# Tiles of the second layer by turns wide and narrow, a gather ring of 63 rows, and graph 2 ranked too, in a two-layer graph network kernel

## The reference

```python
# layer 0
scores = jnp.where(adj != 0, -jnp.arange(N), -jnp.inf)      # the first 25 neighbours
vals, idx = jax.lax.top_k(scores, 25)
agg = jnp.where(valid, x[idx], -inf).max(axis=2)            # elementwise maximum of their rows
agg = jnp.where(degree <= 25, jnp.maximum(agg, 0), agg)     # degree = sum of the adjacency row
x1 = layernorm(x + relu(concat([x, agg]) @ W0 + b0))
# layer 1, 8 heads of 32
Wh = x1 @ W
e = leaky_relu(s1[i] + s2[j] + edge_emb[1], 0.2)            # only where adj[i, j] is 1
alpha = softmax(e over the neighbours)
h = sum_j alpha[i, j] * Wh[j]
out = layernorm(x1 + elu(layernorm(h) * gamma + beta))
```

## Time and profile before

| what | us |
|---|---|
| median of 3 runs (lowest, highest) | 3435.09 (3434.90, 3439.38) |
| the profiled execution, its own time | 3435.9 |
| its span | 3434.2 |
| POOL busy | 2484.3 (72%) |
| DVE busy | 2417.8 (70%) |
| PE busy | 1578.9 (46%) |
| ACT busy | 1114.7 (32%) |
| POOL idle before its ring gathers, put down to "issue" | 705.0, in 2217 pieces |

### The profile page before, as it was taken

The page is one execution under the profiler, slowest core; times in us unless marked ns, Lnnn a source line. Parts: engine busy times, 40 slices in busy tenths (PEclk is TensorE's granted clock), DMA queues, the critical chain, the costliest instruction groups (busy, mean ns, idle before and its releaser), DMA issues. The chain is left out here.

```text
span 3434.2 us, 25542 instructions
## 1 busy us (share of the span) xinstructions
PE 1578.9 (46%) x5123; PEld 1176.3 (34%) x5131; DVE 2417.8 (70%) x5791; ACT 1114.7 (32%) x2307; POOL 2484.3 (72%) x2612
## 2 busy tenths in 40 slices
PE   0036455433563445544365344544454444654354
PEld 0024234322442333333244333433343333443333
DVE  8798789575776767777697766967675545655466
ACT  3224345332343333433344333422222221332134
POOL 2476777777777777777777777777777777777575
PEclk9986667656666666667676676666666666777676
DMA  6657777755576555766568555565544444444232
GB/s 233 215 193 243 260 261 235 227 173 181 174 235 210 183 185 188 249 201 198 173 215 263 187 189 173 179 186 152 152 117 123 115 116 115 120 117 112 74 106 76
DMA packets 221587, 610.01 MB, mean 178 GB/s; under 512 B 68849, under 2 KB 112882, under 8 KB 194802
## 3 DMA queue, kind: packets, MB, share of 16 engines
q0 software_dynamic: 122880, 342.62, 33.6%
q1 hardware_dynamic: 98546, 265.71, 22.7%
HBM read 555.19 MB, written 52.95 MB: 177 GB/s over the span
## 5 line engine op out<-in xcount | busy, mean ns | idle before, releaser
L585 POOL DMA_INDIRECT ring<-table_d,idx_loc x1096 | 1050.3, 958 | 362.6 <-issue 361.4
L585 POOL DMA_INDIRECT ring<-sorted_d,idx_cur x685 | 658.7, 962 | 210.1 <-issue 209.2
L847 PE MATMUL score_p<-ident,x1k 128*128 128x128 f32 x256 | 81.1, 418 | 1406.3 <-ACT x_t L685 1402.5
L875 PE MATMUL att_p<-ring,ident 128*128 128x256 f32 (+1 forms) x2384 | 608.3, 414 | 176.1 <-DVE ring L1297 175.4
L1140 DVE TENSOR_REDUCE agg<-ring 128x256 f32<-128x2560 f32 (+9 forms) x120 | 453.7, 3781 | 207.4 <-DMA ring<-sorted_d,idx_cur 145.2
L875 PEld LDWEIGHTS att_p<-ring,ident 128*128 128x128 f32 (+1 forms) x2384 | 500.7, 212 | 279.4 <-DVE ring L1297 153.2
L847 PEld LDWEIGHTS score_p<-ident,x1k 128*128 128x128 f32 x256 | 35.9, 197 | 1457.0 <-issue 1452.4
L716 ACT ACTIVATE neg<-z 128x256 f32<-128x256 f32 x128 | 53.3, 416 | 1397.9 <-DVE z L1183 1397.9
L585 POOL DMA_INDIRECT ring<-in_x_dram,idx_cur x411 | 392.2, 954 | 130.8 <-issue 124.6
L839 PE MATMUL lin_p<-w_s,h_t 128*128 128x256 f32 x1024 | 471.5, 641 | 0.0
L839 PEld LDWEIGHTS lin_p<-w_s,h_t 128*128 128x128 f32 x1024 | 319.6, 327 | 149.0 <-issue 81.1
(11 more groups left out here) (159 smaller groups left out, 2850.8 us busy)
## 6 DMA issues: line engine op xcount, KB each, us to landing
adj_i<-in_adj_dram SPq DMA_DIRECT2D x208, 1024.0 KB, 5.8
ring<-table_d,idx_loc POOLq DMA_INDIRECT x1096, 2.8
pay<-in_x_dram SPq DMA_DIRECT2D x8, 2048.0 KB, 9.8
xs<-sorted_d SPq DMA_DIRECT2D x128, 128.0 KB, 5.7
ring<-sorted_d,idx_cur POOLq DMA_INDIRECT x685
table_d<-tab SPq DMA_DIRECT2D x80, 132.0 KB, 3.8
ring<-in_x_dram,idx_cur POOLq DMA_INDIRECT x411
sorted_d<-pay,rank_i POOLq DMA_INDIRECT x128, 3.6
```

What stands on the lines that cost most here:

```text
L585: pool.indirect_dma_start(out=to[:, k * width:(k + 1) * width], out_offset=None, in_=source, in_offset=bass.IndirectOffsetOnAxis(ap=idx_at ...
L875: last = pe.matmul(att_p[:, 0:C], ident[0:on, :], r3[0:on, s, 0:C], start=(s == 0), stop=(s == k - 1))
```

## The change

`RANKED` goes from 3 to 2, so that graph 2 is handled like the graphs behind it. The 16 additional degree casts of graph 2 are put into `order_casts`: five between the searches ahead of the rounds, two in each of rounds 0 to 4, one in round 5. `tile1` takes the layer 1 tiles of graphs 0 to 6 in the order 6, 14, 11, 0, 2, 4, 13, 15, 1, 3, 5, 8, 10, 7, 9, 12; graph 7 stays as it is. The ring gets 63 places in place of 55, and 31 tiles of x1 are kept in place of 39.

```diff
-RANKED = 3
+RANKED = 2
...
-RING = 55
-X1_KEPT = 39
+RING = 63
+X1_KEPT = 31
...
+ORDER1 = [6, 14, 11, 0, 2, 4, 13, 15, 1, 3, 5, 8, 10, 7, 9, 12]
...
 def tile1(j):
     b, w = j // T, j % T
-    return b, (w if b == B - 1 else T - 1 - w)
+    return b, (w if b == B - 1 else ORDER1[w])
...
 def order_casts():
-    order = [("search", n) for n in range(AHEAD + 2)]
+
+    first = iter(range(RANKED * T, RANKED * T + T))
+    order = []
+    for n in range(AHEAD + 2):
+        order.append(("search", n))
+        if n >= AHEAD - 3:
+            order.append(("degree", next(first)))
+    before = len(order)
     of_round = []
     for r in range(ROUNDS):
         start = len(order)
         if r + AHEAD + 2 < TILES:
             order.append(("search", r + AHEAD + 2))
-        if RANKED * T <= r + DAHEAD < TILES:
+        for n in [n for n in (next(first, None), next(first, None)) if n is not None]:
+            order.append(("degree", n))
+        if RANKED * T + T <= r + DAHEAD < TILES:
             order.append(("degree", r + DAHEAD))
         of_round.append(range(start, len(order)))
-    return order, of_round
+    return order, before, of_round
...
-            for n in range(T + 4, AHEAD + 4):
+            for n in range(T + 4, CASTS_BEFORE + 2):
                 load_adj(n)
...
-            for n in range(T, AHEAD + 2):
+            for n in range(T, CASTS_BEFORE):
                 cast(n)
```

More of the change, by code:

```diff
@@ L86, in order_casts @@
             order.append(("search", r + AHEAD + 2))
-        if RANKED * T <= r + DAHEAD < TILES:
+        for n in [n for n in (next(first, None), next(first, None)) if n is not None]:
+            order.append(("degree", n))
+        if RANKED * T + T <= r + DAHEAD < TILES:
             order.append(("degree", r + DAHEAD))
         of_round.append(range(start, len(order)))
-    return order, of_round
-CASTS, CASTS_OF = order_casts()
+    return order, before, of_round
+CASTS, CASTS_BEFORE, CASTS_OF = order_casts()
 CAST_AT = {c: k for k, c in enumerate(CASTS)}
```

## The result

The changed kernel takes 3416.4 us (median of 4 runs, 3414.55 to 3418.14) against 3437.24 for the kernel before (4 runs, 3434.90 to 3440.87): a ratio of 0.9937, 95% interval 0.9925 to 0.9949, or 21 us less. The forecast was 3409, range 3392 to 3432: right in direction and within the range, 7 us too low. The profiled execution took 3418.14 us, span 3416.4; the span of before was 3434.2.

What follows compares the result with a forecast made beforehand. POOL's unbroken chain of gathers was taken as the bound behind round 12. From the profiled 3435.9 us, -21.0 (scatters) - 28.1 (stall) + 23.3 (start) gave 3410.1, or 3409 as median; range 3392 to 3432.

Steps and rivals of the forecast that it cites:

- POOL's chain is the bound: Behind round 12 POOL gathers without pause; instructions or stalls taken from it are won in full, other engines' savings nothing.
- Stall of 28.1 us: Between rounds 134 and 135, before graph 7's tile 0 is gathered; the new order removes POOL's wait, winning 28.1 us.
- The price of 0 us for the 8 ring places: The additional ring places loosen only waits that cost POOL under 2 us in all, so they win 0 us.
- 16 table scatters, 21.0 us: Rounds 39 to 54: POOL loses graph 2's 16 table-tile scatters at 1.31 us each, winning 21.0 us.
- the start, 23.3 us: Before round 10: graph 2's earlier loads, casts and ranking delay POOL's chain by 23.3 us, bounds 11.4 and 40.3.
- (a): Ahead of round 0: three degree casts before tile 22's search cast, at 4.0 us per cast, delay DVE by 8.0 us.
- (b): Rounds 1 to 5: nine additional loads make 13.5 us of transfers per 12 us round; 7 us delay, bounds 0 and 20.
- (c): Round 7: graph 2's ranking, formerly covered in round 25, now delays DVE by 8.3 us.
- One sign: Between 170 and 270 us: ACT waiting for loads more than 40 us in total would show the forecast wrong.
- The start costs little: Rival: early loads slip into gaps, delay under 11 us, time about 3394; chance 0.11.
- the start costs more than is won: Rival: loads between 150 and 270 us hold up DVE's searches, delay 72 us, time 3458; chance 0.08 for slower.
- The stall is only moved: Rival: the 28 us stall reappears, for instance at round 48 or 122; time 3437, no difference; chance 0.05.

Runs made afterwards that it cites:

- e1: Kernel before with the new tile order, ring of 63 and 31 tiles of x1, RANKED = 3 and casts as before: 3417.1 us, ratio 0.9921.
- e4: e1 with the old ring of 55 places and 39 tiles of x1: 3416.8 us, ratio 0.9920.
- e9: e6 with table tiles 0 to 7 of graph 0 scattered one round later: 3394.0 us, ratio 0.9872.
- e10: The changed kernel with table tiles 0 to 7 scattered one round later: 3404.0 us, ratio 0.9902.
- e11: e8 with table tiles 0 to 7 scattered one round later: 3398.9 us, ratio 0.9889.
- e5: Kernel before with the new tile order in graph 6 alone, 55 places, 39 tiles of x1, RANKED = 3: 3423.6 us, ratio 0.9958.
- e2: Changed kernel with the old tile order, 55 places and 39 tiles of x1, keeping RANKED = 2 and its casts: 3447.6 us, ratio 1.0009.
- e3: Changed kernel with RANKED = 3, keeping graph 2's 16 additional loads and degree casts but not its early ranking: 3431.8 us, ratio 0.9964.
- e6: e1 with the loads of adjacency tiles 20 and 21 issued ahead of graph 0's lists and graph 1's rows: 3406.4 us, ratio 0.9910.
- e7: Changed kernel with graph 2's 16 degree casts moved ahead among graph 0's and later searches, none in the rounds: 3413.6 us, ratio 0.9931.
- e8: e7 with loads up to the search of tile 21 issued ahead of graph 0's lists: 3410.1 us, ratio 0.9923.

## Why the prediction was right, point by point

**POOL's chain is the bound.** Shown, by e1 (a gap of 28.1 us gone, 27.3 won), e4 (a ring that no one waits for, no change), and e9 to e11 (11.2, 13.7 and 10.9 us of POOL's waits for table tiles taken away; 11.8, 12.2 and 10.6 won).

**Stall of 28.1 us.** Measured 27.3 in e1 and 27.6 in e4, each within some 4.6 us. In e1's profile POOL's time from the end of round 12 to the end of the last scatter is 29.5 us shorter than before (3059.2 and 3088.8), and the end of the program 3.6 longer. The price of 0 us for the 8 ring places holds with this order; e5 shows that the lay of the ring decides whether the order wins all of it.

**16 table scatters, 21.0 us, against the start, 23.3 us.** Their balance was forecast as +2.3 and measured as +3.2 in e2. The start in its terms, from the times in the table at e3 and the profile of the changed kernel:

| term | forecast | measured |
|---|---|---|
| (a) ahead of round 0 | 8.0 | 9.1 at the mark (174.90, was 165.80), 9.0 at round 1 (202.8, was 193.8) |
| (b) rounds 1 to 6 | 7 | 6.7 (round 7 at 281.5, was 265.8: 15.7 - 9.0) |
| (c) the ranking | 8.3 | 8.2 on POOL's side, 8.9 in DVE's round 7 |
| POOL, end of round 12 | 23.3 | 25.4 (366.5, was 341.1) |

The pace of 4.0 us per cast was 4.1 (172.86 - 152.45 over five). Of the signs named ahead, the mark (174.9, forecast 174), round 7 (281.5, forecast 281) and the table waits (46.9, forecast 44) came as said, and so did the engine share but for one stretch (0.92 to 0.97, and 0.79 from 248 to 260; forecast 0.85 or more). The last gather ended 21.4 us earlier and not 26.

One sign spoke against the forecast. ACT waited for loads between 170 and 270 us for 33.2 us before degree casts and 17.7 before search casts, 50.9 in all, where more than 40 were to show it wrong. The delay stayed within its bounds because only a part of these waits reached DVE, and by a path that term (b) did not name. Behind 175 us DVE never waited for a search cast. But in ACT's program the copies for PE (`h_t`) and the square root (`std`) of a round stand behind the casts. ACT and then DVE at the head of round 4:

```profile
237.23 1.91 ACT L679 ACTIVATE adj_h<-adj_i 128x2048 bf16<-128x2048 int32 x1 [3.34 <-DMA adj_i<-in_adj_dram]
...
239.66 0.20 ACT L736 ACTIVATE std<-var 128x3 f32<-128x3 f32 x1
```

```profile
239.90 0.18 DVE L1187 RECIPROCAL rstd<-std 128x3 f32<-128x3 f32 x1 [1.39 <-ACT std L736]
```

DVE's waits between 202 and 282 us, of which the kernel before has neither:

```profile
DVE z L1272 <- PE lin_p L853: 4.4, 3, 1.7
DVE rstd L1187 <- ACT std L736: 2.6, 2, 1.4
```

Together they are 7.0 us, the 6.7 of term (b). They lie in rounds 3 to 6 (1.2, 2.2, 1.6 and 1.5 us longer than before); rounds 1 and 2 are not longer, though the DMA engines are as full there. So the size of (b) was right and its rule, transfers beyond 12 us in each of rounds 1 to 5, only roughly. DVE waited for no gather between 137 and 345 us.

Two readings of the prediction were off without weight. The wait of 5.78 us at 319.82 is not POOL's last for a table tile: one of 1.81 us follows at 364.32, and it is 2.23 after the change. And with 2.65 or 2.9 us per tile in the sum of term (b) it gives 3 or 5 us, not 5 or 6.

**The step that was mis-sized** is the sum: the profiled execution went down by 17.8 us and not by 25.8. 2.1 us are the longer start. 2.3 us are missing between the end of round 12 and the end of the last scatter: POOL took 3041.9 us for it in place of 3088.8, 46.8 less, where 21.0 + 28.1 = 49.1 were forecast. And 3.6 us stand behind the last scatter, a term that the sum did not have: the scatter's end lies 4.4 us ahead of the span's end before and 8.0 us after. In that time the trace has a drain of POOL, of 4.17 us before and 7.76 after (8.06 in e1, 4.07 in e2). SP's wait for the others at the end of the program grows with it, before and after:

```profile
SPq L161 <- PEq L161: 1.1, 1, 1.1
```

```profile
SPq L175 <- PEq L175: 4.8, 1, 4.8
```

Every kernel with the new order in at least graph 6 has the 8.0 us (e1 and e3 to e11), e2 with the old order has 4.3. Why the order of tiles should lengthen POOL's last drain stays open. The 2.3 us are covered by the scatters of results, 1028 ns each in place of 1001, times 128: 3.4 us. They too go with the order: 1019 to 1040 ns in the nine other kernels that have it in graphs 0 to 6, 1011 and 1012 in e2 and e5; why was not tried. Against the medians, 20.8 us less, the error is 5 us.

**The rivals.** "The start costs little" is refuted by e2 and e3, and "the start costs more than is won" by the result. Taken against the 21.0 us of the scatters alone, though, the start does cost more (25.4, and e2). "The stall is only moved" is refuted for the change, and came true in e5, at a place that the prediction had not named.

## What to carry to other kernels

A busy share of 72% can be a full engine: look for a constant gap between its instructions, and price every edit by the instructions and stalls that it takes from that engine. Where a bound engine waits for a slower neighbour only at the start, move the thing it waits for one step later before making the neighbour faster; here an edit of four lines of that kind gave 11 to 12 us on each of three kernels, while the earlier loads of e6 gave 4. Work moved out of a full stretch into another stretch pays only if the resource it needs there is free, so look up that stretch's DMA share before.

## What the runs showed of the hardware that was not expected

Full DMA engines did not slow POOL's issue here: between 224 and 236 us of the changed kernel, at a share of 0.92, ten gathers took 9.26 us of busy time, and 9.24 in the kernel before at 0.59. The end of the program behind the last scatter, in which the trace has POOL's drain, took 3.6 us longer in each kernel in which layer 1's tiles of graph 6 were reordered, for the same instructions at the end; the cause is open.
